# Norm's power and the gate weights earlier in the expert stages, and the gate's column products ahead of sigma's second products

## The reference

```python
x = x + _L0_conv_ref(_ln_c(x), ...)   # stage 0: gate, rank-1 softmax attention over pixels
t = t + _L0_ffn_ref(_ln_t(t), ...)    # stage 1: top-k tokens through a gelu layer
x = x + _L1_conv_ref(_ln_c(x), ...)   # stage 2: deformable 3x3 convolution
t = t + _L1_ffn_ref(_ln_t(t), ...)    # stage 3: 8 experts, top 2, softmax weights
x = x + _L2_conv_ref(_ln_c(x), ...)   # stage 4: squared cosine similarity attention
t = t + _L2_ffn_ref(_ln_t(t), ...)    # stage 5: 8 experts, top 2, weights renormalised
x = x + _L3_conv_ref(_ln_c(x), ...)   # stage 6: 3x3 convolution, kernel / sigma
t = t + _L3_ffn_ref(_ln_t(t), ...)    # stage 7: 8 experts, a layer norm of their own, top 2
```

```python
sim = x0[:, :, None] * x1[:, None, :]
feats = jnp.einsum('bn,bnm->bm', x2, jax.nn.softmax(sim, axis=1))
gate = jax.nn.sigmoid(feats)
```

## Time and profile before

| what | us |
|---|---|
| median of 3 runs | 1166.83 |
| lowest and highest | 1162.14, 1176.15 |
| profiled execution | 1172.36 |
| its span | 1170.6 |
| TensorE busy, with 4266 matmuls | 951.9 |
| DVE, ACT, POOL busy | 697.0, 493.2, 445.8 |

### The profile page before, as it was taken

How to read it: one execution, slowest core, us unless ns; L and a number is a source line. 1 busy time by engine, 2 the same in 40 slices (tenths; PEclk the granted TensorE clock), 3 DMA queues, 4 the chain that set the end, 5 groups by cost and what they waited for, 6 DMA issues and landing times.

```text
span 1170.6 us, 16680 instructions
## 1 busy us (share of the span) xinstructions
PE 951.9 (81%) x4266; PEld 567.0 (48%) x4266; DVE 697.0 (60%) x2439; ACT 493.2 (42%) x966; POOL 445.8 (38%) x1234
## 2 busy tenths in 40 slices
PE   2656387758998998989888777799988767999998
PEld 2545265435554555555534434465554554444443
DVE  2876676746455664554467756656675554566653
ACT  1322222245445654552445445333343012666664
POOL 4565566631543535446244221134564321111100
PEclk9999996659889988998789887857779666999999
DMA  4500000000000000000000000000000000000000
GB/s 74 86 0 1 0 1 0 0 1 1 1 1 0 0 0 0 1 1 1 1 0 1 0 0 1 1 0 0 0 1 0 1 0 0 5 5 4 9 5 9
DMA packets 26352, 6.21 MB, mean 5 GB/s; under 512 B 24068, under 2 KB 26244, under 8 KB 26308
## 3 DMA queue, kind: packets, MB, share of 16 engines
q1 hardware_dynamic: 26308, 5.70, 2.8%
HBM read 4.65 MB, written 1.05 MB: 5 GB/s over the span
## 4 chain that ended last, share of the span: by engine, by line
PE 44%; issue 16%; DVE 10%; POOL 5%; ACT 4%; DVEq 0%; POOLq 0%; ACTq 0%; another core or an unknown queue 0%
PE banks L1449 8%; PE banks L1275 6%; PE banks L1158 5%; PE banks L1159 3%; PE banks L1089 3%; PE banks L1466 2%; PE banks L1473 2%; PE banks L1267 2%; PE banks L1417 2%; DVE weighted L1994 1%; DVE summed L1998 1%; DVE V L1720 1%; PE banks L1263 1%; PE banks L1230 1%; POOL rstd L646 1%
## 5 line engine op out<-in xcount | busy, mean ns | idle before, releaser
L962 ACT ACTIVATE scratch<-banks,b 128x512 f32<-128x512 f32 x224 | 144.3, 683 | 57.2 <-PE banks L1159 45.1
L1449 PE MATMUL banks<-scratch,W 128*64 128x512 f32 (+1 forms) x448 | 151.8, 661 | 0.4
L1889 DVE TENSOR_TENSOR scratch<-banks,XR 128x1024 f32<-128x1024 f32 x72 | 87.5, 1224 | 87.3 <-PE banks L1267 61.1
L1158 PE MATMUL banks<-VS,W_hi 128*128 128x512 f32 x240 | 120.6, 503 | 2.1 <-DVE X L2067 1.0
L646 POOL TENSOR_TENSOR rstd<-vareps,neghalf 128x4 f32<-128x4 f32 x64 | 66.8, 1044 | 128.6 <-DVE vareps L1708 124.0
L1159 PE MATMUL banks<-VS,W_lo 128*128 128x512 f32 x240 | 106.4, 443 | 0.0
L1994 DVE SCALAR_TENSOR_TENSOR weighted<-banks,b,cwide 128x512 f32<-128x512 f32 x72 | 53.9, 748 | 73.7 <-PE banks L1449 72.9
L1275 PE MATMUL banks<-scratch,region 128*64 128x256 f32 x576 | 88.0, 432 | 3.0 <-DVE scratch L1889 3.0
L1720 DVE TENSOR_SCALAR V<-X,moments,rstd 128x64 f32 (+1 forms) x256 | 67.6, 328 | 36.7 <-POOL rstd L646 32.6
L973 ACT ACTIVATE cwide<-banks 128x512 f32<-128x512 f32 x96 | 57.4, 598 | 73.8 <-PE banks L1466 73.5
L1132 PE MATMUL banks<-ident,V 128*128 128x128 f32 x128 | 33.7, 354 | 58.5 <-DVE V L1720 58.4
(11 more groups left out here) (289 smaller groups left out, 2039.6 us busy)
## 6 DMA issues: line engine op xcount, KB each, us to landing
W<-in_L_ffn_W SPq DMA_DIRECT2D x3, 512.0 KB
X<-in_x SPq DMA_DIRECT2D x8, 128.0 KB, 2.7
out<-X SPq DMA_DIRECT2D x8, 128.0 KB, 2.0
cwide<-in_L_ffn_W SPq DMA_DIRECT2D x2, 256.0 KB
KC<-in_L_conv_kernel SPq DMA_DIRECT2D x2, 144.0 KB
W<-in_L_ffn_W SPq DMA_DIRECT2D x1, 256.0 KB
cwide<-in_L_ffn_w SPq DMA_DIRECT2D x2, 128.0 KB
Ko<-in_L_conv_w SPq DMA_DIRECT2D x1, 144.0 KB, 3.7
```

Of the source, the lines that this page charges most:

```text
L962: act.activation(hid[:, c % 4, :], bank[c % 2][:, :], ACT.Gelu, bias=b1[s][:, w:w + 1]).then_inc(h_ready, 1)
L1158: pe.matmul(out, hi, VS[u][:], start=True, stop=False)
L1449: ins = pe.matmul(y, W2[s][:, w, :], hid[:, c % 4, :], start=opens, stop=closes, skip_group_check=True)
L1889: vec.tensor_tensor(S[:, k % 3], pair(p), xr, ALU.mult).then_inc(s_ready, 1)
```

## The change

Three edits to the order of work; no instruction is added or left out.

1. POOL: in the expert stages the norm's power comes ahead of `powers`. The second power of stage 7 keeps its place behind it, as `prep_token`.
2. DVE: `prep_norm` is split into `prep_values` and `prep_token`. In the expert stages `prep_values` moves from behind weight 1 to ahead of it. In stages 5 and 7 `weigh` moves to the same place, from behind weight 2. In stage 7 `prep_token` (XN) stays between weights 1 and 2, while V and the second statistics go with `prep_values`.
3. TensorE: in the first half of a pair of the gate stage, `gate_cols` comes directly behind `gate_rows` and ahead of `slot2`. In the second half nothing moves.

```diff
--- before.py
+++ after.py
@@ -644,6 +644,8 @@
                     return
                 pool.wait_ge(var_ready, b + (NB * s + 1))
                 pool.tensor_tensor(rstd[:], vareps[:], neghalf[:], ALU.pow).then_inc(rstd_ready, 1)
+
+            def prep_token(b, s):
                 if s == 7:
                     pool.wait_ge(var2_ready, b + 1)
                     pool.tensor_tensor(rstd[:], vareps[:], neghalf[:], ALU.pow).then_inc(rstd2_ready, 1)
@@ -664,12 +666,16 @@
                     second_half = step is not None and (u == 1 or s == 2)
                     if s == 2:
                         seg1(step)
-                    if s in MOE and (u == 0 or not wrap):
-                        powers(i * 2 + (MOE0[s] + u + 1), s)
                     if u == 0:
                         prep(i * 2 + 2 - wrap, s_next)
                     elif not wrap:
                         prep(i * 2 + 3, s)
+                    if s in MOE and (u == 0 or not wrap):
+                        powers(i * 2 + (MOE0[s] + u + 1), s)
+                    if u == 0:
+                        prep_token(i * 2 + 2 - wrap, s_next)
+                    elif not wrap:
+                        prep_token(i * 2 + 3, s)
                     if s != 2 and first_half:
                         seg1(step)
                     if first_half:
@@ -713,6 +719,7 @@
                 if s in MOE:
                     powers(MOE0[s], s)
                 prep(1, s)
+                prep_token(1, s)
                 if s == 0:
                     front()
                     rewind()
@@ -1187,10 +1194,9 @@
                         pe.wait_ge(vt_ready, b + 2)
                         pe.wait_ge(block_done, b + 2)
                         gate_rows(1 - u)
+                        gate_cols(1 - u)
                     if u == 0:
                         slot2(i + STEP0[s], bank[7])
-                    if u == 0 or not wrap:
-                        gate_cols(1 - u)
                     prep_ahead(prep, i, u, s, s_next, wrap)
 
             def topk_stage(i, s, s_next, wrap):
@@ -1713,6 +1719,10 @@
                 stats_of(lambda t: X[:, bass.ds(b * NT + t, 1), :].rearrange("p o c -> p (o c)"), EPS_OF[s], var_ready)
 
             def prep_norm(b, s, u):
+                prep_values(b, s, u)
+                prep_token(b, s, u)
+
+            def prep_values(b, s, u):
                 vec.wait_ge(rstd_ready, b + (NB * s + 1))
                 vec.wait_ge(v_turned, b + (NB * s + 1))
                 for t in range(NT):
@@ -1723,6 +1733,9 @@
                 if s == 7:
                     vec.wait_ge(v_ready, b + (NB * s + 1))
                     stats_of(lambda t: V[u][:, t, :], EPS_T, var2_ready)
+
+            def prep_token(b, s, u):
+                if s == 7:
                     vec.wait_ge(rstd2_ready, b + 1)
                     if not isinstance(b, int) or b:
                         vec.wait_ge(xn_turned, b)
@@ -2024,10 +2037,13 @@
                     weight(i, 0, s, u)
                     if s == 5:
                         link(vec.tensor_tensor(xblock(b), xblock(b), V[u][:], ALU.add))
+                    ahead(prep_values, i, u, s, s_next, wrap)
+                    if more and s != 3:
+                        weigh(m + 1, s, 1 - u)
                     weight(i, 1, s, u)
-                    ahead(prep_norm, i, u, s, s_next, wrap)
+                    ahead(prep_token, i, u, s, s_next, wrap)
                     weight(i, 2, s, u)
-                    if more:
+                    if more and s == 3:
                         weigh(m + 1, s, 1 - u)
                     weight(i, 3, s, u)
                     ahead(prep_split, i, u, s, s_next, wrap)
```

## The result

The changed kernel takes 1132.77 us (median of four runs, 1126.02 to 1135.47); the kernel before took 1167.55 (four runs beside it, 1162.14 to 1176.15). The ratio is 0.970, with a 95% interval of 0.967 to 0.974. The forecast was 1130, within 1113 to 1151. The profiled executions took 1172.36 before and 1133.36 after, 39.0 less, against a sum of 43; the medians lie 34.8 apart, since the profiled execution before lies 4.8 above its median.

The account below looks back on a forecast made before the run. No engine is full, so loops of handovers and TensorE's clock bound the kernel: gate 10.4, first expert stage 12.5, second 3.5, their clock 9 and 8 sum to 43 us off 1172.4, so 1130 us, range 1113 to 1151.

Parts of the forecast that it names:

- The gate stage: Column products ahead of sigma's second products start the exponentials 3.4 us earlier; a pair takes 22.35, not 25.04; 10.4 us gained.
- The third rival: Gate stage pays only its transposes, 6.9, first expert stage V alone, 7, clock as before: 1157 us; chance 0.05.
- 12.5 forecast for seven turns of 1.8: Stage three, order: earlier norm power and V bring `cw` 1.8 us earlier in seven turns; 12.5 us.
- 9 forecast: Stage three, clock: with less standing at the turn TensorE's clock stays up, 4.8 plus four times 1.0; 9 us.
- 11.5 forecast: Stage five in all: 3.5 us from the order and 8 us from the clock.
- with the blocks at 14.8 where the clock holds: Stage five: VectorE bounds full-clock blocks, busy 11.98 of 14.81 us, its operations only reordered.
- 3.5 forecast, of it 2 at half clock: Stage five, order: 0.5 us in each of four half-clock blocks, 1 to 2 in one more; 3.5 us.
- two of three blocks would stay up: Stage five, clock: two of three falling blocks keep full clock, 4 us each beyond the order's 0.5; 8 us.
- The split of the wait: Stage five: the 2.17 us wait for `cw` becomes 1.1 before the fourth second product and 1.1 before the turn back.
- The first (clock doesn't follow, 1146): Rival: clock falls come as often at other places; only 26.4 us of order gains remain, 1146 us; chance 0.27.
- The second (all falls go, 1120): Rival: all falls go, also in stage five and the first pair; 52 us gained, 1120 us; chance 0.12.
- The fourth, the bank of weight 1 as the bound: Rival: V and `weigh` delay weight 1's bank, lengthening turns in stages three, five, seven by 46 us: 1196; chance 0.03.

Follow-up runs that it names:

- The gate's part alone: Kernel before with only TensorE's column products of the gate moved ahead of sigma's second products, expert stages as before: 1158.37 us, ratio 0.991.
- POOL's order alone: Kernel before with only the norm's power moved ahead of the gate weights' power on POOL in the expert stages: 1144.83 us, ratio 0.978.
- the filled kernel: Kernel before plus two idle 128x512 TensorE products in stages three and five where it waited for `cw`, no order changed: 1151.71 us, ratio 0.988.
- the experts alone: Changed kernel without the gate stage's edit, so only the POOL and VectorE edits of the expert stages: 1135.76 us, ratio 0.973.
- stage seven put back: Changed kernel with VectorE's old order in stage seven, V behind weight 1 and `weigh` behind weight 2: 1132.81 us, ratio 0.969.
- POOL's old order: Changed kernel with the norm's power again behind the gate weights on POOL in stages five and seven, stage three keeping the new order: 1135.57 us, ratio 0.968.
- with the block's end filled: Changed kernel plus two idle 128x512 products in stage five before the turn back, where TensorE waits for the sum: 1130.06 us, ratio 0.969.
- with all waits filled: Changed kernel plus, in stage five, one idle 128x512 product behind sigma's small products and two before the turn back: 1131.73 us, ratio 0.965.
- one product in the thin place: Changed kernel plus one idle 128x512 product behind sigma's small products in stage five, nothing else: 1141.65 us, ratio 0.979.

## Why the prediction was right, and where its terms were off

**The gate stage** was right in mechanism and size: the exponentials came 3.34 us earlier (3.4 forecast), a pair took 22.56 (22.35), and the stage gave 10.9 (10.4). The gate's part alone gave 10.4 by its ratio. The third rival, a gain of the transposes alone, is out.

**The first expert stage**, order: 12.5 forecast for seven turns of 1.8. The `cw` wait was forecast at 1.2 and is 1.20. The kernel before with its clock held takes 15.87 a block, the changed one 14.05, so a turn gives 1.8; between the first and the last end that made 11.0. The seventh turn lies in the stage's first part, which gave 2.0, but that part is 33 to 42 us long in profiled executions whatever the order, so I can't tell it there. What I had not seen is whose edit it is: POOL's order alone gives it all. I had V "written before weight 1" as a part of the path; it is not.

**The first expert stage**, clock: 9 forecast, 9.4 measured with nothing but idle products in the kernel before. That the falls there come from the standing at the turn is shown: filled, or shortened from 2.23 and 0.74 to 1.20, it left the clock at 1.00 in every block. The Trainium skill ("TensorE: Matmul & The Clock Gate", section "Why this matters for your kernels") asks for no long gap between bursts of matmuls; in stage three these runs agree in kind, but the waits that brought the clock down there, 2.23 us with 0.74 a little before it, are shorter than the gaps that its table warns of. In stage five the rule doesn't cover what was measured: a block with no wait in it, behind one with 0.13 us of idle time, fell to a clock of 0.59.

**The second expert stage** is where two terms were wrong and partly made up for it: 11.5 forecast, 6.6 measured. The step that failed is the length of a block at full clock ("with the blocks at 14.8 where the clock holds"), taken as VectorE's bound. The block of 14.81 had a clock of 0.93; its end ran at 1.2 GHz. With the clock held, the order of before takes 13.95 and the changed one 14.11. For the long blocks no window of the old order stands at 1.00; an estimate from the one of 16.29 at 0.90 in the filled kernel, less half of the 3.4 us at half clock, is some 14.6, beside 14.49 with the change. So the new order is worth about nothing at full clock (3.5 forecast, of it 2 at half clock), and the 6.6 go with the clock. There I forecast that two of three blocks would stay up. Of the three of 67 products two did (14.49 and 13.81 in place of 19.47 and 19.18: 5.0 and 5.4), and the first short one as well (14.50 for 19.12: 4.6). But two falls now last a whole block: 23.54 for 19.48 and 18.87 for 14.82, 4.1 lost each. With the small rest (0.7 gained in the third, 0.9 lost in the last) this is the 6.7 of the stage's ends. The gain of 4.6 and the first loss of 4.1 also stand in the kernel with the gate's part alone (14.40 and 23.47), which has the old order in stage five, so these two are not that order's. The premise was wrong as well: by the earlier trace rows I took the falls to follow the wait of 2.17, but in the kernel with the filler there they also come behind waits of 0.68 at most. That two of the three blocks stayed up came true, but the runs don't bear out the reason given for it, and the new fall in a short block was not forecast; so the 6.6 of the 11.5 are in good part luck.

**The split of the wait** was right in kind. The bank's wait is 0.99 (1.1 forecast) but comes only in two short blocks. The one before the turn back is 1.83 there, not 1.1, and 1.23 and 0.55 in the long blocks at full clock. The bank's wait is hidden, as forecast: moving `weigh` away took it out and gained at most 0.2 us in a block.

**The rivals.** The first (clock doesn't follow, 1146) fails in stage three, by 9.4 us, and is half true in stage five. The second (all falls go, 1120) fails in stage five. The fourth, the bank of weight 1 as the bound, makes TensorE wait 2.37 in a block of stage three when POOL's order is left as it was. The change escapes it by moving POOL's work as well.

**What stays open** is what brings the clock down in stage five. The falls come at the same blocks in four kernels that share VectorE's and TensorE's order there (the changed one, the experts alone, stage seven put back, POOL's old order), so they are not chance from one execution to the next. But the order of stage five alone doesn't fix them: with the old order there, the kernel before and the one with the gate's part alone differ in the first two blocks. What comes ahead of the stage matters too. The other orders and fillers moved the falls or changed their number, and none took them all away. No version that was tried can be told from the changed kernel for the better.

## What to carry to other kernels

When a step on one engine is moved ahead, first see that the engine that feeds it has delivered by then: V ahead of weight 1 made stage three's blocks 19.3 instead of 16.9 us with POOL's old order (a part of it the clock's), and cost nothing with the new one, which alone gave stage three's gain. Price the clock apart from the order, with a few idle products in the wait of the unchanged kernel: here it split 20.5 us into 9.4 and 11.0. And take a block's length "at full clock" only from a window whose granted clock is 1.00, since 0.93 hid 0.9 us in 14.81.

## What was not expected of the hardware

In stage five TensorE's clock stayed at 1.2 GHz for about 17 to 24 us of work without a wait: 23.54 us busy of 23.54 at a clock of 0.51. In the changed kernel that fall began just behind the wait of 1.83 us. But standing doesn't explain the falls: with the block's end filled the clock fell behind 4.47 us in which TensorE was busy throughout, and with all waits filled one fall was left, in a block busy for 25.17 of 25.17 us. And a fill in part only (one product in the thin place) gave more falls than none, 124.3 us for the stage against 111.1, each in one profiled execution.
